# A middle stage that keeps x and h in SBUF, finds row ids by one-hot products, and gathers rows on POOL

## What is computed

```python
sa, ca, ga, sb, cb, gb = split(silu(c) @ wmod)         # ga, gb: magnitude at least 0.25
h = layernorm(x) * (1 + ca) + sa
q, k, v = heads(h @ w_qkv)
q = softmax(q * SCALE, axis=-1); k = softmax(k, axis=tokens)
context = einsum('hnd,hne->hde', q, k)
x = x + ga * (merge(einsum('hde,hnd->hne', context, v)) @ w_out + b_out)
h = layernorm(x) * (1 + cb) + sb
p = softmax(h @ Wg + bg); keep the two largest per token, divided by their sum + 1e-8
x = x + gb * sum_e p_e * (gelu(h @ W1[e] + b1[e]) @ W2[e] + b2[e])
```

## Time and profile before

| what | value |
|---|---|
| median of 3 runs | 966.51 us (966.34 to 971.07) |
| profiled execution, its own time | 965.11 us |
| its span in the trace | 963.4 us |
| PE busy (weight loads apart) | 825.7 us, 86% |
| DVE, ACT, POOL busy | 572.3, 455.7, 276.9 us |
| mean granted clock of PE | 0.928 |

### The profile page before, as it was taken

One profiled execution on the slowest core, in us unless ns is written; L12 is line 12 of the kernel. 1 busy time (PEld: TensorE's weight loads), 2 busy tenths in 40 slices (PEclk: granted clock), 3 DMA queues, 4 the chain that ended last, 5 costly groups with the idle time before them and its releaser, 6 DMA issues.

```text
span 963.4 us, 17833 instructions
## 1 busy us (share of the span) xinstructions
PE 825.7 (86%) x5866; PEld 765.9 (80%) x5867; DVE 572.3 (59%) x1365; ACT 455.7 (47%) x876; POOL 276.9 (29%) x206
## 2 busy tenths in 40 slices
PE   5757999999998869864049999999998999999995
PEld 4545888888886757664049999999998999999995
DVE  4768677777777436886016565556656565565553
ACT  4343555665543420111036565747457575665552
POOL 1222223322321012277713222222222222232222
PEclk9979999999998987875569999999999999999998
DMA  8601101101100096643632425152242524322222
GB/s 288 221 0 45 40 5 46 44 1 45 45 1 1 1 348 223 236 153 107 228 108 62 115 40 132 27 132 44 44 131 44 131 44 115 61 45 44 44 45 33
DMA packets 51260, 84.77 MB, mean 88 GB/s; under 512 B 4498, under 2 KB 35668, under 8 KB 51092
## 3 DMA queue, kind: packets, MB, share of 16 engines
q1 hardware_dynamic: 37396, 65.62, 20.1%
q0 software_dynamic: 13824, 18.65, 10.8%
HBM read 50.86 MB, written 33.40 MB: 87 GB/s over the span
## 4 chain that ended last, share of the span: by engine, by line
PE 71%; DVE 12%; POOL 5%; issue 5%; DMA 3%; ACT 1%; SPq 1%; DVEq 0%; ACTq 0%; POOLq 0%
PE ps L1318 20%; PE ps L1306 16%; PE ps L1147 9%; PE ps L1112 8%; PE ps L1166 6%; POOL lists L539 4%; PE ps L1223 3%; PE ps L1156 3%; PE ps L1289 2%; DVE w_lo L1054 2%; DMA listed<-lists 2%; DMA wmod_sb<-in_L_wmod 1%; PE ps L1217 1%; DVE w_lo L1051 1%; DVE ln_s L766 1%
## 5 line engine op out<-in xcount | busy, mean ns | idle before, releaser
L559 POOL DMA_INDIRECT out<-y,y_id x74 | 122.2, 1651 | 349.1 <-DVE y L1043 334.7
L1318 PE MATMUL ps<-w_hi,hid_hi 128*128 128x256 f32 x592 | 171.2, 289 | 12.2 <-DVE hid_lo L1034 12.2
L715 ACT ACTIVATE hid<-ps,b_col 128x256 f32<-128x256 f32 x296 | 122.2, 464 | 113.0 <-PE ps L1306 112.9
L1034 DVE TENSOR_TENSOR hid_lo<-hid,hid_hi 128x512 fp32r<-128x512 f32 x148 | 100.6, 692 | 117.8 <-ACT hid_hi L723 116.4
L1306 PE MATMUL ps<-xT_hi,w_hi 128*128 128x256 f32 x592 | 167.5, 283 | 2.3 <-DVE xT_lo L1015 2.3
L1306 PE MATMUL ps<-xT_lo,w_hi 128*128 128x256 f32 x592 | 167.3, 283 | 0.0
L1306 PE MATMUL ps<-xT_hi,w_lo 128*128 128x256 f32 x592 | 167.2, 282 | 0.0
L1318 PE MATMUL ps<-w_hi,hid_lo 128*128 128x256 f32 x592 | 166.1, 281 | 0.0
L1318 PE MATMUL ps<-w_lo,hid_hi 128*128 128x256 f32 x592 | 166.1, 281 | 0.0
L1318 PEld LDWEIGHTS ps<-w_hi,hid_hi 128*128 128x128 f32 x592 | 112.1, 189 | 15.6 <-DVE hid_lo L1034 14.7
L514 POOL TENSOR_TENSOR q_n<-q_exp,q_rec 128x1024 f32<-128x1024 f32 x32 | 61.0, 1906 | 218.3 <-DVE q_rec L790 218.3
(11 more groups left out here) (190 smaller groups left out, 1491.4 us busy)
## 6 DMA issues: line engine op xcount, KB each, us to landing
w_raw<-in_L_ffn_W SPq DMA_DIRECT2D x16, 1024.0 KB, 8.8
listed<-lists SPq DMA_DIRECT2D x38, 265.0 KB, 3.0
h_store<-h_q SPq DMA_DIRECT2D x8, 1024.0 KB, 4.0
h_b<-h_store SPq DMA_DIRECT2D x16, 512.0 KB, 6.2
x_all<-in_L_attn_x SPq DMA_DIRECT2D x8, 512.0 KB, 11.0
x_b<-in_L_attn_x SPq DMA_DIRECT2D x4, 1024.0 KB, 10.4
out<-x SPq DMA_DIRECT2D x8, 512.0 KB, 3.2
lists<-pad SPq DMA_DIRECT2D x8, 265.0 KB, 2.4
```

The costliest lines, as they stand in the source:

```text
L559: pool.indirect_dma_start(out[:, :], bass.IndirectOffsetOnAxis(ap=y_id[:, i:i + 1], axis=0), y[:, i, :], None, compute_op=ALU.add).then_in ...
L715: ins = act.activation(hid[:, m, :], ps[:, k, (m % 2) * BT:(m % 2 + 1) * BT], ACT.Gelu_apprx_tanh, bias=b1_col[:, bass.ds(e, 1), m])
L1034: dve.tensor_tensor(hid_lo[:, m, :], hid[:, m, :], hid_hi[:, m, :].bitcast(F32), ALU.subtract).then_inc(s_hid, 1)
L1318: last = pe.matmul(ps[:, Y0 + i, 0:D], a, w, start=m == 0 and st, stop=m == M - 1 and sp_)
```

## The change

- x and h stay in SBUF from the first stage on (`x_all`, `h_all`): no `h_store`, and no group loads. POOL adds the bias of w_out to `x_all` during attention (`add_bias`, eight times).
- `attend` is four float32 products of 256 columns per pair. `residual` adds them into `x_all`. PE transposes the plain x, and the layer norm is applied to the logits instead (`scale`; wg_mod has its column means removed). ACT normalises the rows in place (`normal`), and SP writes them to the DRAM array `xrows` in token order.
- Routing runs in two halves of 16 tiles. The steps of the first stand between the residuals of pairs 8 to 15.
- A list place is cut into a high part (place >> 7) and a low part. For chunks of four tiles, one-hot matrices of both are made (`at_hi` with token - N in it, on POOL, or on DVE for chunks 4 and 6; `at_lo` on DVE for odd chunks and on ACT for even ones), and 64 products of [128 x 128] by [128 x 256] add up to the token id in each place. DVE adds N; places without a token get ids of padding rows (`ids`).
- In the expert stage POOL copies two columns of `ids` and gathers the two halves of a block from `xrows` into `listed`, in place of SP's load; the loop is written with the gather of block n+2 ahead of the scatter of block n. y_id is copied by POOL, not by DVE. SP keeps only the weight loads. An expert has at least three blocks.

```diff
 SP
+            def load_weights(e):
+                sp.dma_start(w1_raw[:, :, :], W1[e, :, :].rearrange("(c p) n -> p c n", p=P)).then_inc(s_wraw, 16)
+                sp.dma_start(w2_raw[:, :, :], W2[e, :, :].rearrange("(m p) n -> p m n", p=P)).then_inc(s_wraw, 16)
...
-            def expert(e, par, nb, last):
-                load_rows(e, 0)
-                with sp.Fori(1, nb) as b:
-                    load_rows(e, b)
-                if not isinstance(e, int):
-                    wait_reg(s_wlo, e + 2)
...
+            load_weights(1)
+            sp.wait_ge(s_idxr, 1)
             sp.dma_start(b2_bc[:, :, :].rearrange("p e d -> p (e d)"), b2.rearrange("e d -> (e d)").partition_broadcast(P)).then_inc(s_b2, 16)
...
+            for e in range(2, E):
+                sp.wait_ge(s_wlo, e)
+                load_weights(e)
...
 POOL
+            def hi_hot(c):
+                g, cc = divmod(c, GCH)
+                pool.wait_ge(s_lohi, g + 1)
+                after(pool, s_idx, c - GCH + 1)
+                for k in range(2):
+                    for i in range(CH):
+                        last = pool.tensor_scalar(at_hi[:, cc, k, i, :], iota_hi[:, :], spot_hi[:, g, k, cc * CH + i:cc * CH + i + 1],
+                                                  token_of[:, c * CH + i:c * CH + i + 1], ALU.is_equal, ALU.mult)
+                last.then_inc(s_hiP, 1)
...
+            def gather(col, n):
+
+                pool.wait_ge(s_meta, n + ONE)
+                pool.wait_ge(s_bt, n + ONE)
+                pool.sem_inc(s_turn_pool, 1)
+                pool.tensor_copy(gid[:, :], ids[:, bass.ds(col, BI)]).then_inc(s_gid, 1)
+                pool.wait_ge(s_gid, n + 1)
+                pool.sem_inc(s_turn_pool, 1)
+                for i in range(BI):
+                    pool.indirect_dma_start(listed[:, i, :], None, xrows[:, :],
+                                            bass.IndirectOffsetOnAxis(ap=gid[:, i:i + 1], axis=0)).then_inc(s_rows, 16)
+
+            def scatter(col, gv):
+
+                pool.wait_ge(s_added, gv * 32 + DMA2)
+                pool.sem_inc(s_turn_pool, 1)
+                pool.tensor_copy(y_id[:, :], ids[:, bass.ds(col, BI)]).then_inc(s_yid, 1)
+                pool.wait_ge(s_yid, gv + 1)
+                for i in range(BI):
+                    pool.wait_ge(s_y, gv * 2 + (i + 1 + TWO))
...
             def expert(e, par, nb, last):
-                with pool.Fori(0, nb) as b:
+                with pool.Fori(0, nb - 2) as b:
                     gv = now(pool, g)
...
+                    gather(e * COLS + b * BI + 2 * BI, gv + 2)
+                    scatter(e * COLS + b * BI, gv)
                     pool.reg_add(g, g, 1)
...
 DVE
-            link(dve.tensor_tensor(fold[:, :, :], ps[:, 4:6, 0:D], bc(gates[:, 0, :], 1, [P, C, D]), ALU.mult))
-            link(dve.tensor_copy(fold_hi[:, :, :], fold[:, :, :]))
-            dve.tensor_tensor(fold_lo[:, :, :], fold[:, :, :], fold_hi[:, :, :].bitcast(F32), ALU.subtract).then_inc(s_foldr, 1)
...
+            dve.tensor_tensor(fold[:, :, :], ps[:, 4:6, 0:D], bc(gates[:, 0, :], 1, [P, C, D]), ALU.mult).then_inc(s_foldr, 1)
...
+            for q in range(PAIRS):
+                residual(q)
+                if q == 8:
+                    spread(0)
+                if q == 9:
+                    root(0)
+                if q == 10:
+                    scale(0)
+                    first(0)
...
+                if q == 14:
+                    lo_hot(1)
+                if q == 15:
+                    lo_hot(3)
...
+            place(1)
+            hi_hot(4)
+            lo_hot(5)
+            count_blocks()
+            hi_hot(6)
+            lo_hot(7)
...
                     dve.wait_ge(s_added, gv * 32 + DMA2)
-                    link(dve.tensor_copy(y_id[:, :], listed_id[:, :]))
 PE
+            def attend(q):
+
+                after(pe, s_x1, 2 * q - 4)
+                for i in range(2):
+                    t = 2 * q + i
+                    for c in range(C):
+                        last = pe.matmul(ps[:, AT + q % 3, i * D:(i + 1) * D], h_all[:, c, t * P:(t + 1) * P], fold[:, c, :],
+                                         start=c == 0, stop=c == C - 1)
...
+                for k in range(2):
+                    for i in range(CH):
+                        last = pe.matmul(ps[:, IX, 0:E * COLS], at_lo[:, cc, k, i, :], at_hi[:, cc, k, i, :],
+                                         start=c == 0 and k == 0 and i == 0, stop=c == CHUNKS - 1 and k == 1 and i == CH - 1)
```

More of the change, by code:

```diff
@@ L34 @@
 BI = BT // P
-CAP = N + BT
-ROW = D + E + 1
+COLS = N // P
+ROW = D + E
 MAXB = N // BT
+MINB = 3
 EPS = 1e-5
@@ L246, in adaln_block @@
         s_x = [sem(f"s_xin{i}") for i in range(SBN)]
-        s_hst = [sem(f"s_hst{i}") for i in range(HB)]
         s_kev = sem("s_kev")
@@ L876, in _ @@
             dve.wait_ge(s_qn, TILES)
-            for b in range(HB):
-                dve.wait_ge(s_hst[b], 16 * len(range(b, SBN, HB)))
-            dve.memset(ctx_n[:, :, :], 0.0)
             for h in range(2):
@@ new lines, in _ @@
+            dve.wait_ge(s_bo, SBN)
+            dve.wait_ge(s_const, CONSTS)
+            dve.wait_ge(s_iota, IOTAS)
+            for q in range(PAIRS):
+                residual(q)
+                if q == 8:
+                    spread(0)
+                if q == 9:
+                    root(0)
+                if q == 10:
+                    scale(0)
+                    first(0)
+                if q == 11:
+                    second(0)
+                if q == 12:
+                    weigh(0)
+                if q == 13:
+                    place(0)
+                if q == 14:
+                    lo_hot(1)
+                if q == 15:
+                    lo_hot(3)
@@ new lines, in _ @@
+            spread(1)
+            root(1)
+            scale(1)
+            first(1)
+            second(1)
+            weigh(1)
+            place(1)
[4 more added lines that the diff above has]
+            lo_hot(7)
+            dve.wait_ge(s_idx, CHUNKS)
+            link(dve.scalar_tensor_tensor(pad_t[:, :], ps[:, IX, 0:E * COLS], 0.0, pad_row[:, :], ALU.is_ge, ALU.mult))
+            dve.scalar_tensor_tensor(ids[:, :], ps[:, IX, 0:E * COLS], float(N), pad_t[:, :], ALU.add, ALU.add).then_inc(s_idxr, 1)
@@ L1179, in _ @@
                     q_mm(s + 1, j // 2, (j % 2,))
[L1180 to L1181 removed]
+                if s == SBN - 1 and j in (5, 6):
+                    half = j - 5
                     if half == 0:
@@ L1281, in _ @@
+            for q in range(AHEAD):
+                attend(q)
+            for q in range(PAIRS):
+                rows_T(q)
+                if q + AHEAD < PAIRS:
+                    attend(q + AHEAD)
+                logits(q)
+                if q == 12:
+                    ranks(0)
+            index(0)
+            index(1)
+            index(2)
+            ranks(1)
+            for c in range(3, CHUNKS):
+                index(c)
             pe.wait_ge(s_counts, 1)
```

636 lines of the change are left out of this document (328 added, 308 removed).

## The result

The changed kernel takes 1048.11 us (median of 4 runs, 1046.85 to 1050.17) where the kernel before, timed beside it, took 966.42: a ratio of 1.0835, 95% interval 1.0797 to 1.0874. It was forecast at 960.

A forecast was written before the change was run, and what follows sets the result against it. It took matmuls to bound the expert stage and POOL's 64 scatters the middle one; -54.2 + 31.8 + 1.2 + 13.2 + 2 = -6.0 us against 965.1 gave 959.1, said as 960, range 925 to 984.

The forecast's parts named there:

- The fold: Between fold and attention: one multiply of 512 columns left, 0.9 us with handover, -2.4 us; attention starts at 355.7, full clock.
- the eight bias additions: Attention: they lie in POOL's idle time, costing zero, and up to 2 us if DVE is held by them.
- The residual loop: Middle stage, 16 pairs: TensorE takes 3.1 us a pair, DVE's routing keeps up, and the loop ends at 404.1.
- The high one-hots: Middle stage: POOL's 128x256 `tensor_scalar` taken as 0.5 us; chunks 5 and 7 take 8.0 us, to 425.2, hidden.
- Rival 5: Middle stage: POOL's one-hots take twice 0.5 us each, chunks 5 and 7 end 8 us later: 968, chance 0.10.
- The first gather: End of middle stage: second landing 6.8 us after its issue, at 437.4; first expert product at 440.8.
- An expert's first block: Expert stage: weight loads hold the gathers, +31.8 us for six experts, +1.2 for the seventh, +13.2 for the lowered clock.
- The other blocks: Expert stage: a new loop through POOL takes 11.8 us against a period of 11.73; 29 blocks x 0.07, +2 us.
- Rival 4: Expert stage: POOL's loop becomes the bound if a gather issue costs 1.85, not 1.26 us: 985, chance 0.15.
- Two blocks ahead moves no read earlier: Expert stage: `listed` is still one buffer, so gather(n+2) waits until block n+1's y_w is copied and its transposes done.

The follow-up runs named there:

- x4: The changed kernel without the eight additions of the output bias on POOL during attention (output lacks b_out): 1041.83 us.
- x7: The changed kernel with twelve more POOL instructions ahead of its one-hots, to read the durations of different instruction forms: 1050.5 us.
- x11: The changed kernel without the weight loads of experts 2 to 7, which compute with expert 1's raw weights: 1030.46 us.
- x9: The changed kernel with POOL's scatters of block n ahead of the gathers of block n+2: 1101.69 us.
- x1: The changed kernel with DVE copying a block's weights out of `listed` one block earlier, into a second tile: 952.39 us, ratio to before 0.9858.
- x3: The changed kernel with the high one-hots of chunks 1, 2 and 5 moved from POOL to DVE: 1028.73 us.
- x5: The changed kernel with the edits of x1 and x3 together: 930.52 us, ratio 0.9346 to a kernel before of 997.0 us.
- x12: The kernel before with x1's edit, weights and ids of a block copied out of `listed` one block early: ratio 0.9966.
- x6: x5 with the bias additions moved to DVE's wait for the fold and the padding stores before POOL's one-hots: 925.10 us, ratio 0.9291.

## Why the prediction was wrong, point by point

Forecast -6 us, measured +81.7. By its own steps:

- **The fold: right in kind, cover mis-sized.** The first residual is released as said (PE idle 0.78 us, expected 0.9; clock 1.00, as expected). But "the eight bias additions lie in POOL's idle time: zero, and up to 2 us" was at least 3.6 by x4: attention started at 360.28, not 355.7.
- **The residual loop: right.** 16 pairs took 49.9 us (360.28 to the last residual at 410.21), expected 48.4. PE is busy for 46.7 of the 48 us from 360 to 408.
- **The high one-hots: the step that failed first.** "Its 128x256 tensor_scalar is in no row; I take 0.5, nearer the upper." It takes 1.21 at the median and 1.30 on the mean. The upper end, 0.57, came from the earlier trace rows, which are another form (two full operands, one operation) of eight times the columns, in which a fixed part is spread thin: 256 columns of that form take 0.75 (x7). It was no bound. 48 of them are 62 us, and with PE's queue they also held the rank counts. The ids came at 473.3, not 428.7. Rival 5 named the mechanism and priced it at a fifth, for two reasons: it took 1.0 us an instruction, and it counted only the 16 of chunks 5 and 7, where the 32 of chunks 0 to 3 stand ahead of them on POOL. At 1.0 us each, 48 from 407.93 would have ended at 456, not 8 us behind 425.2.
- **The first gather: too dear.** "Second landing 6.8 after its issue", as beside a weight load: 3.02 us beside the load of b2.
- **An expert's first block: mechanism right, sizes not.** The gathers beside a weight load landed in 5.0 to 6.2 us (6.8 expected, 2.8 without), and PE ran at a clock of 0.50 for some 5.6 us behind the first of these waits (511.9 to 517.5; 4.4 expected). The Trainium skill, "DMA: Bandwidth & Descriptors", section "Issuing engines are not separate DMA queues", has the two share engines; the trace agrees: the second gather took 5.58 us in place of 2.8, with the DMA share at 1.02. x11 prices this at 2.9 us a load. But the first two distances of seven experts lost 59 us in sum (5.3 + 2.2 for six and 1.2 forecast: 46). The missing part is the loop: before, the block behind w_lo caught up (8.9 us), while now no distance between two y_w is under 13.06, so w_lo adds itself in full (17.9 and 13.4 in x11, which has no loads).
- **The other blocks: the step that cost most.** "11.5 us, 11.8 with 0.3 for POOL's branches, against a period of 11.73", and so +2. The loop is 13.34. Its terms, forecast and measured: y to the end of y_w 1.84 and 2.01; to the first gather's start 0.70 and 1.46; two gathers 2.52 and 2.31; to the first scatter 0.35 and 1.35; scatter to scatter 1.85 and 2.22; landing 4.2 and 3.99. The hand-overs made it: 0.85 to 0.93 us pass between a copy and the indirect DMA that uses it, even on POOL itself, and I had put 0 to 0.35, for which no row stands in the forecast. The two terms with such a copy are 1.76 us of the 1.88 by which the sum of 11.46 was short. The trace of before shows that price, in DVE's row behind the first of the earlier trace rows and POOL's ahead of the earlier trace rows:
```profile
535.15 0.49 DVE L1043 SCALAR_TENSOR_TENSOR y<-y,y_w,gates 128x256 f32<-128x256 f32 x1
```
```profile
536.53 1.54 POOL L559 DMA_INDIRECT out<-y,y_id  x1 [8.33 <-DVE y L1043]
```
  y's first half ends at 535.64 and its scatter starts 0.89 us later. I read only the 0.30 between two DMAs of one queue. The other 22 distances should have cost 2 us and cost 34.
- **Rival 4** ("POOL's loop becomes the bound", 0.15) is what happened, for another reason: a gather's issue is 1.03, not 1.85. Its price of 985 was low because it took 20 blocks, and because it stood alone; the forecast treated POOL late in the middle and POOL late in the loop as rivals, and both came.
- **"Two blocks ahead moves no read earlier"** was right (x9, x1), but its consequence was drawn only for the reads, not for the loop.

## What to carry to other kernels

When a step moves to another engine, write down the loop that it closes, term by term, with a row for each hand-over and not only for each instruction; a loop that comes out at the period itself, as here (11.8 against 11.73), is not hidden. A buffer's release should stand directly behind its last necessary reader: one small copy, made 5 us earlier, turned 1.08 times the time of before into 0.99 (1048.1 and 952.4 us). A price for an instruction form that no row shows is bounded by measuring that form, not by a wider or simpler one.

## What the runs showed of the hardware

- POOL's `tensor_scalar` on 256 float32 columns takes 1.22 us, DVE's 0.43 (x7, x3).
- Some small DVE operations are longer while POOL makes one-hots: of those of 128 columns, one in every 1.2 us takes 0.53 in place of 0.29 us (421.06, 422.28, 423.49), and 1.2 us is the length of a one-hot on POOL. None of them does so in the first half, with POOL idle. No run tests the cause. The same instruction of the first half, with POOL idle, and of the second, beside POOL's one-hots (DVE of the changed kernel):
```profile
387.55 0.17 DVE L845 TENSOR_SCALAR bn_i<-bn_v 128x16 int32<-128x16 int32 x1
...
414.96 0.49 DVE L845 TENSOR_SCALAR bn_i<-bn_v 128x16 int32<-128x16 int32 x1
```
- The kernel before took 966 us where it was timed beside the changed kernel and x1 to x4, and 997 to 1000 us on the two chips of x5 to x12. The changed kernel shows no such difference: x7, on one of those chips, took 1050.5, with twelve more instructions on POOL, behind which POOL still waited 6.7 us for DVE. x12's trace has its first y_w at 529.8, not 495.8, and then blocks as usual. SP's eight small stores of padding take 38.68 us there:
```profile
476.62 38.68 SPq L452 DMA_DIRECT2D lists<-pad  x8
```
In the kernel before, on the first chip, they took 15.36. In x12's trace the chain of waits runs over SP there, in steps of 0.7 us. Why is open. So x6's ratio of 0.929 is partly this; against 966 it would be 0.957.
